# A fused block of feed-forward, attention and feed-forward: tiles of the head normalised one slot ahead, and a projection moved to another row of the plan

## The reference, cut to what matters

```python
def ffn(x, weight, bias):
    scale = mean(abs(weight))
    w_t = clip(round(weight / (scale + 1e-10)), -1, 1)      # ternary weights
    return einsum('bsi,oi->bso', x, w_t * scale) + bias
def attn(x, Wqkv, bqkv, Wo, bo):                            # 16 heads of 32
    kqv = (x @ Wqkv + bqkv).reshape(b, s, 3, 16, 32)
    q, k, v = kqv[:, :, 0], kqv[:, :, 1], kqv[:, :, 2]
    scores = triu(einsum('bsnh,btnh->bnst', k, q) / sqrt(32)) + -10000.0 * tril(ones, k=-1)
    out = einsum('bnkq,bknh->bqnh', softmax(scores, axis=2), v)
    return out.reshape(b, s, 512) @ Wo + bo
x = x + 0.5 * ffn(layernorm(x), ffn_weight, ffn_bias)       # x is (4, 1024, 512), fp32
x = x + attn(layernorm(x), Wqkv, bqkv, Wo, bo)
x = x + 0.5 * ffn(layernorm(x), ffn_weight, ffn_bias)
```

## Time and profile before

| | before |
|---|---|
| median of 3 runs | 1333.44 us (1330.6 to 1333.57) |
| the profiled execution's own time | 1330.46 us |
| its span | 1328.7 us |
| mean granted TensorE clock | 0.977 |
| PE busy | 1232.6 us (93%) |
| DVE busy | 831.3 us (63%) |
| ACT busy | 502.9 us (38%) |
| POOL busy | 349.2 us (26%) |

### The profile page before, as it was taken

One profiled execution on the slowest core, in us unless ns is written; L12 is line 12 of the kernel. 1 busy time (PEld: TensorE's weight loads), 2 busy tenths in 40 slices (PEclk: granted clock), 3 DMA queues, 4 the chain that ended last, 5 costly groups with the idle time before them and its releaser, 6 DMA issues.

```text
span 1328.7 us, 27193 instructions
## 1 busy us (share of the span) xinstructions
PE 1232.6 (93%) x10938; PEld 752.7 (57%) x10938; DVE 831.3 (63%) x2048; ACT 502.9 (38%) x1139; POOL 349.2 (26%) x492
## 2 busy tenths in 40 slices
PE   3569999899999999999999999999999999998886
PEld 2456656455656566565656565665656565664454
DVE  5545446579754666779754666769854666755444
ACT  1111444344443434344443434344443434343521
POOL 3541111025400222325401222325401231300233
PEclk9688899999999999999999999999999999999998
DMA  7322211111011201221111101221111101000110
GB/s 237 103 74 79 91 53 37 38 52 54 34 33 64 66 25 57 102 73 60 41 34 64 66 26 57 96 73 65 41 34 64 65 26 57 33 18 10 41 49 32
DMA packets 40685, 77.26 MB, mean 58 GB/s; under 512 B 5232, under 2 KB 10352, under 8 KB 40560
## 3 DMA queue, kind: packets, MB, share of 16 engines
q1 hardware_dynamic: 40560, 75.52, 16.9%
HBM read 49.81 MB, written 25.17 MB: 56 GB/s over the span
## 4 chain that ended last, share of the span: by engine, by line
PE 83%; DVE 11%; issue 3%; ACT 2%; DMA 1%; POOL 0%; SPq 0%; DVEq 0%; ACTq 0%
PE bank L963 29%; PE bank L1023 11%; PE bank L1045 10%; PE bank L1067 10%; PE bank L988 8%; PE bank L1078 8%; PE bank L980 4%; PE bank L1051 3%; DVE st L699 2%; DVE hn L710 2%; DVE mst L739 2%; ACT prob L896 1%; DVE xt L730 1%; DVE junk L745 1%; DVE rec L756 1%
## 5 line engine op out<-in xcount | busy, mean ns | idle before, releaser
L896 ACT ACTIVATE prob<-bank 128x512 f32<-128x512 f32 (+3 forms) x768 | 314.7, 496 | 309.7 <-PE bank L1051 309.2
L745 DVE CUSTOM_DVE_ANT_0 junk<-bank,mask 128x384 bf16<-128x384 f32 (+3 forms) x512 | 220.4, 487 | 139.7 <-PE bank L1023 139.1
L739 DVE TENSOR_REDUCE mst<-bank 128x1 f32<-128x512 f32 x256 | 158.8, 682 | 121.0 <-PE bank L1023 121.0
L963 PE MATMUL bank<-hT,wqk 128*128 128x512 f32 x768 | 194.5, 402 | 0.0
L1045 PE MATMUL bank<-qT,kT 32*128 32x512 f32 (+2 forms) x2304 | 183.9, 381 | 11.4 <-DVE mst L739 5.9
L650 POOL TENSOR_SCALAR_AFFINE_SELECT prob<-prob 128x512 f32<-128x512 f32 x128 | 81.6, 638 | 429.0 <-ACT prob L896 428.9
L1023 PE MATMUL bank<-kT,qT 32*128 32x512 f32 (+2 forms) x2304 | 181.8, 383 | 3.0 <-DVE mst L739 1.7
L1023 PEld LDWEIGHTS bank<-kT,qT 32*128 32x128 f32 x2304 | 102.5, 183 | 133.5 <-issue 98.9
L963 PEld LDWEIGHTS bank<-hT,wqk 128*128 128x128 f32 x768 | 141.4, 190 | 40.8 <-issue 7.6
L1078 PE MATMUL bank<-prob,ones 128*32 128x512 f32 (+3 forms) x1536 | 159.0, 486 | 0.0
L1045 PEld LDWEIGHTS bank<-qT,kT 32*128 32x128 f32 x2304 | 104.3, 183 | 89.4 <-issue 45.8
(11 more groups left out here) (76 smaller groups left out, 1118.5 us busy)
## 6 DMA issues: line engine op xcount, KB each, us to landing
wqk<-weight_scratch SPq DMA_DIRECT2D x30, 512.0 KB, 3.3
wvo<-weight_scratch SPq DMA_DIRECT2D x20, 512.0 KB, 5.9
xt<-in_L_attn_x_dram SPq DMA_DIRECT2D x32, 256.0 KB, 3.6
residual_scratch<-xt SPq DMA_DIRECT2D x32, 256.0 KB, 2.0
xt<-residual_scratch SPq DMA_DIRECT2D x32, 256.0 KB, 3.4
out_dram<-xt SPq DMA_DIRECT2D x32, 256.0 KB, 2.0
o<-in_L_attn_Wqkv_dram SPq DMA_DIRECT2D x12, 256.0 KB, 3.9
weight_scratch<-o SPq DMA_DIRECT2D x6, 512.0 KB, 2.9
```

Source lines behind the costliest of these rows:

```text
L739: nc.vector.tensor_reduce(mst[:, 1, at:at + 1], psum(u, h), AX, ALU.max).then_inc(ring_free, 1)
L745: nc.vector.tensor_tensor_reduce(junk[:, turn % 2, 0:n], psum(u, h)[:, 0:n], mask[:, CW - n:CW], 1.0, -3e38, ALU.add, ALU.max, mst[:, 2 * ...
L896: nc.scalar.activation(prob[:, at % 2, h, off:CW], psum(("S", b, n), h)[:, off:CW], ACT.Exp, scale=SCALE)\
L963: m = nc.tensor.matmul(psum(u), left(x, k), right(y, k), start=(n == 0), stop=(n == len(terms) - 1))
```

## The change

In the head, `normal` and `add_bias` of a slot's tiles are issued one slot earlier, on DVE and on POOL. In all later slots they stay where they were. In the tables of `FIRST_ROWS` and groups 0 to 2 the four `P` of a group stand in rows 0, 1, 2, 3 in place of rows 0, 1, 3, 4; the third one now shares row 2 with `M`. To make room, `F2.2` goes from row 2 to row 4 of group 1 and `F2.7` from row 2 to row 3 of group 2. `GROUP3_ROWS`, `LAST_ROWS`, `TAIL_ROWS` and `HEAD_ROWS` are as before. SP's list follows the tables: it issues the load of the next `wqk` half (L526) and the store of an F2 tile in the slots to which those uses went.

```diff
 GROUP0_ROWS = (
     "P | A | LO",
     "P | A",
-    "M | A",
+    "M P | A",
     "P | A | X3.0",
-    "P | A | X3.1",
+    " | A | X3.1",
     "O.0 | A | X3.2",
...
 GROUP1_ROWS = (
     "P | A",
     "T3.2 P | A",
-    "M F2.2 | A",
+    "M P | A",
     "P | A | X3.5",
-    "P | A",
+    "F2.2 | A",
     "T3.3 O.5 | A | X3.6",
...
 GROUP2_ROWS = (
     "P | A | X1.0",
     "P | A | X1.1",
-    "M F2.7 | A | X1.2",
-    "T1.0 P | A | X1.3",
-    "T1.1 F1.0 P | A | X1.4",
+    "M P | A | X1.2",
+    "F2.7 T1.0 P | A | X1.3",
+    "T1.1 F1.0 | A | X1.4",
     "T1.2 F1.1 | A | X1.5",
...
 FIRST_ROWS = (
     "P | A",
     "P | A | | W",
-    "M | A",
+    "M P | A",
     "P | A | | W",
-    "P | A",
+    " | A",
     "V.4 | A | | W",
...
+NORMALISED = [[u for n, s in enumerate(SLOTS) if n - (s.b < 0) == k for u in s.uses() if u in TURN]
+              for k in range(len(SLOTS))]
...
@@ gpsimd @@
-                for u in s.uses():
-                    if u in TURN:
-                        add_bias(u)
+                for u in NORMALISED[k]:
+                    add_bias(u)
...
@@ vector @@
-                for u in s.uses():
-                    if u in TURN:
-                        normal(u)
+                for u in NORMALISED[k]:
+                    normal(u)
```

## The result

The changed kernel took 1316.74 us (median of 4 runs, 1310.41 to 1320.51) against 1332.59 for the kernel before (4 runs, 1330.6 to 1333.57), a ratio of 0.988, 95% interval [0.984, 0.992]. Measured again beside the experiments it was 1317.88 us and 0.989 [0.987, 0.991]. So it is faster by 1.2%; forecast was 1.8%, 1309.5 us, with 1301 to 1320 as the range. The profiled execution took 1315.88 us, its span is 1313.7.

A forecast was written before the change was run, and what follows sets the result against it. The prediction took the head to be bound by a chain in which PE and DVE take turns. 1330.46 - 23.5 (head) + 1.8 (moved P) = 1308.8 us profiled, 1309.5 as median, range 1301 to 1320.

The forecast's parts named there:

- The chain of the head: 20 to 100 us: PE and DVE take turns; issuing a slot ahead cuts a turn from 6.9 to 9 us to 5.5 to 5.9.
- loop of 4.9: Head, one slot: residual, statistics, POOL's pair, both `normal`, both low parts; 4.9 us, longer where POOL holds `normal` up.
- PE's wait for `hn`: Head, before the transposes: a sign of the forecast, to fall from 34.6 to about 7 us.
- PE's share: Head, first transposes to V.0: a sign of the forecast, PE's busy share to go above 0.8.
- The head's term: Start of the kernel up to V.0: a gain of 23.5 us, V.0 at 76.6 instead of 100.1.
- The port: Head: POOL splits delay `normal` 0.9 to 1.5 us; as rival, each moved `add_bias` does too, +10.4 us, 1320, chance 0.12.
- rival 2: Head: low parts wait behind a `normal` waiting for POOL, the turn stays near 6.9 us; 1321 us, chance 0.09.
- The moved P: Long stage: P moved to row 2 removes one wait and adds another; sum +1.8 us, bounds -4 and +14.
- the wait at row 3: Row 3's scores behind a bare `M` take 1.31 us, covered 0.63; the 0.68 lost goes.
- the one at row 5: Row 5's scores behind the emptied row 4 take 2.27 us instead of 0.97; 1.30 lost.
- A bare group: Groups where nothing covers the emptied row 4: net +0.6 us in each of five.
- Rival 4: Emptied rows drop PE's clock to 1.2 GHz, 3.5 us in each of 11 groups; 1345.5 us, chance 0.04.

The follow-up runs named there:

- e4: e1 plus matmuls whose result is never read, behind every bare row and at other places where PE waits; 1300.49 us, 0.976 of the kernel before.
- e1: The kernel before with only the head's edit (`normal` and `add_bias` one slot earlier) and the old row tables; 1306.88 us, 0.981 of the kernel before.
- e5: e1 with POOL's weight splits of slots 3, 4, 7 and 9 one slot later, behind the bias adds; 1306.44 us, 0.980 of the kernel before.
- e0_after: The whole change measured again, unaltered, beside the kernel before; 1317.88 us, 0.989 of the kernel before.
- e3: The whole change plus matmuls whose result is never read, behind bare rows and before T1.1 in group 2; 1310.15 us.

## Why the prediction was right, point by point, and the step that failed

- **The chain of the head**: right, and its turn right in size, in part by luck. I had 5.5 to 5.9 us from a loop of 4.9 through DVE and POOL with a delay of 0.9 to 1.5 at the port, which by its own terms makes 5.8 to 6.4. Measured were 5.8, but in the slots with a split the chain runs through POOL's list alone, whose 5.6 I had summed and not compared with the turn. PE's wait for `hn` was to fall from 34.6 to some 7 us and fell to 15.6. The head's matmuls became shorter too: PE is busy 39.5 us with the same work instead of 47.9, at a clock of 0.88 instead of 0.79. Since PE isn't the pace, that time turned into waiting, and PE's share stayed at 0.71: e4 has 7 us less at half rate ahead of V.0 than e1, and its V.0 starts only 0.8 us sooner. So the 24.3 us are 19.0 of waits and 8.4 of shorter matmuls, less some 3 of new waits for low parts. Start of T2.0 predicted 34.2, measured 35.2; T2.1 39.7, 41.0; T2.2 45.6, 46.8; T2.3 52.1, 53.8; T2.4 57.9, 59.6; T2.5 65.5, 65.9; T2.6 71.8, 71.0; V.0 76.6, 75.8. The head's term was 23.5 and is 24.3.
- **The port**: `normal` is held up as counted (two of them 1.86 us behind a split), but e5 shows that it isn't the pace; the delay takes time out of a wait for `rstd`.
- **The round trip of POOL** (rival 2) exists as a wait of 0.2 to 1.1 us a slot, inside the loop as I had summed it.
- **The moved P**: the wait at row 3 went, by 0.67 us (0.68 said), the one at row 5 came, 1.42 (1.30 said). A bare group is +0.35 (row 2 +2.76, row 3 -0.67, row 4 -3.16, row 5 +1.42) where I had 0.6. Group 2 of batches 1 and 2 is -0.9 (-1.1), of batch 3 +0.9 (+1.2), and T1.1's wait is 1.38 as before. The sum is +0.6 where I had +1.8.
- **The clock of the long stage: the step that failed.** My sum carried no term for it. Rival 4 named the mechanism, "bare rows drop the clock", at 3.5 us in each of 11 groups, and I gave it 0.04 on the ground that six bare rows in a row had kept a clock of 1.00. They did in that one execution; in e1's, the last of the same six rows is at half rate. It happens in some groups and in some executions, 9.4 us in the profiled one. That is more than the 7.1 by which it missed my 1308.8: without it the execution would have taken 1306.5, and e1, which has less of it, is at 1306.9. So the median fell into the range, but the long stage grew by 9.7 us where the prediction itself called more than 5 wrong. Rival 4 was right in kind and not in place: 4.8 of the 9.4 us stand behind a newly bare row, the rest where the old rows can lose it too. Which stretches fall differs between executions, and what decides it is open. The point from which rival 4 would decide was 2.1 us per changed group, counted for 11 groups; the tables change three in each batch, 12, and the long stage's growth is 0.8 on the mean of 12.

The Trainium skill, "TensorE: Matmul & The Clock Gate", Part 1, says that the monitor behind the clock runs free of the kernel's start. The traces agree as far as they can: the same program lost the clock in row 5 of batch 1, group 0, in both profiled executions, but in that row of batch 0, groups 0 and 1 (140.6 and 208.9 us), only in e0_after's; its runs spread over 10 us while the slots that kept the clock agree to 0.1 us.

## What to carry to other kernels

When the list of one engine makes two engines take turns, issue the producer of the next turn ahead of the consumers of this one; then add up the new loop, since a third engine's list is often just behind. Moving matmuls into one row takes them out of another: an emptied row costs its wait once and, on PE, now and then the clock of the work behind it, so look at the clock column of several executions before calling a stretch safe. Where PE must wait anyway, matmuls that compute nothing can keep its clock. They were free where they were shorter than the wait, and cost 1.0 us over five short rows of the last group.

## What the runs showed of the hardware that I had not expected

- A drop to 1.2 GHz came at a wait of 1.3 to 1.4 us between stretches of dense matmuls (batch 1, group 0, row 5), with PE "busy" 3.40 of 3.40 us by the profile. The same wait in batches 2 and 3 kept 2.4 GHz.
- With four matmuls of 512 columns, 1.19 us, in that wait the clock was 2.4 GHz at every filled place in e3's trace (29 slots, three of them with two matmuls, and three T1.1 with six).
- One and the same program took 1310.4 us at a mean granted clock of 0.979 and 1320.5 at 0.974. That isn't a fixed rate: in another five runs 0.974 went with 1317.6 to 1318.9. Two stretches of 3.4 us more at half rate cost 3.3 us.
